# Causal softmax attention with heads of 8 channels: scores of two steps issued together, masked in PSUM, transposes two steps behind

## What is computed

```python
q, k, v = split((layernorm(x)) @ w_attn + b_attn)   # 16 heads of 8 channels
q, k = rope(q), rope(k)                             # pairs (2n, 2n+1) rotated
att = einsum("bhqd,bhkd->bhqk", q, k) / sqrt(8)
att = where(causal, att, -inf)                      # 256 x 256 for each of 256 (b, h)
y = einsum("bhqk,bhkd->bhqd", softmax(att), v)
x = x + y @ w_proj + b_proj
```

## Time and profile before

| | before |
|---|---|
| median of three runs | 2302.54 us |
| the profiled execution's own time | 2294.92 us |
| its span | 2293.1 us |
| mean granted TensorE clock, share of full | 0.978 |
| busy: TensorE / VectorE / ScalarE / GpSimd | 93% / 74% / 79% / 62% |
| the stage of the change, first S to last S | 209.1 to 523.3 us |

### The profile page before, as it was taken

How to read it: one execution, slowest core, us unless ns; L and a number is a source line. 1 busy time by engine, 2 the same in 40 slices (tenths; PEclk the granted TensorE clock), 3 DMA queues, 4 the chain that set the end, 5 groups by cost and what they waited for, 6 DMA issues and landing times. The chain is left out here.

```text
span 2293.1 us, 67424 instructions
## 1 busy us (share of the span) xinstructions
PE 2136.7 (93%) x22342; PEld 1585.6 (69%) x22342; DVE 1706.8 (74%) x4362; ACT 1801.0 (79%) x6112; POOL 1431.8 (62%) x1432
## 2 busy tenths in 40 slices
PE   6997999998797999999999999898999999999999
PEld 4994666665795888854888854674788864788863
DVE  5565999996555899964899964675899963899964
ACT  4775999995676999973999973556999982999982
POOL 3663777774662888840888850671788850788850
PEclk8997999999899999999999999999999999999999
DMA  6111000000113000000000000000000000000000
GB/s 249 44 42 42 2 0 0 0 1 38 35 44 111 12 7 9 7 3 3 11 7 9 7 0 0 2 0 6 9 9 8 8 1 5 9 9 7 9 1 37
DMA packets 22568, 46.02 MB, mean 20 GB/s; under 512 B 5344, under 2 KB 13664, under 8 KB 22048
## 3 DMA queue, kind: packets, MB, share of 16 engines
q1 hardware_dynamic: 17440, 34.07, 4.4%
q0 software_dynamic: 4992, 10.23, 1.6%
HBM read 24.51 MB, written 11.40 MB: 16 GB/s over the span
## 5 line engine op out<-in xcount | busy, mean ns | idle before, releaser
L280 POOL TENSOR_TENSOR space<-space 128x512 f32<-128x512 f32 x256 | 325.8, 1273 | 270.4 <-DVE space L383 270.1
L275 POOL TENSOR_TENSOR space<-space 128x512 f32<-128x512 f32 x256 | 267.6, 1045 | 128.1 <-ACT space L316 127.6
L330 ACT ACTIVATE space<-psum,space 128x128 f32<-128x128 f32 x1024 | 337.0, 385 | 2.7 <-DVE space L374 2.7
L177 PE MATMUL psum<-big,space 128*128 128x256 f32 x1024 | 267.9, 384 | 7.3 <-issue 3.5
L269 POOL TENSOR_TENSOR space<-space 128x512 f32<-128x512 f32 x256 | 267.0, 1043 | 7.9 <-DVE space L354 7.3
L1008 POOL TENSOR_TENSOR space<-space 128x256 f32<-128x256 f32 (+1 forms) x256 | 221.9, 888 | 75.2 <-DVE space L1117 70.9
L374 DVE TENSOR_REDUCE space<-psum 128x4 f32<-128x512 f32 x256 | 177.1, 692 | 100.8 <-PE psum L192 96.5
L1053 ACT ACTIVATE space<-space 128x128 f32<-128x128 f32 (+1 forms) x512 | 226.1, 446 | 7.3 <-DVE space L1108 6.5
L330 ACT ACTIVATION_READ_ACCUMULATOR space<-psum,space 128x1 f32 x1024 | 201.8, 197 | 0.0
L177 PEld LDWEIGHTS psum<-big,space 128*128 128x128 f32 x1024 | 175.6, 191 | 29.6 <-issue 16.2
L677 ACT ACTIVATE big<-psum,wt 128x512 f32<-128x512 f32 (+1 forms) x96 | 65.4, 686 | 151.9 <-PE psum L654 151.9
(11 more groups left out here) (194 smaller groups left out, 5425.8 us busy)
## 6 DMA issues: line engine op xcount, KB each, us to landing
big<-early SPq DMA_DIRECT2D x1, 6944.0 KB, 27.9
rows<-space SPq DMA_DIRECT2D x16, 256.0 KB, 2.7
z<-token_y SPq DMA_DIRECT2D x16, 256.0 KB, 4.7
space<-z SPq DMA_DIRECT2D x64, 64.0 KB, 1.9
space<-z SPq DMA_DIRECT2D x64, 63.8 KB, 2.1
big<-late SPq DMA_DIRECT2D x1, 3114.0 KB, 13.7
x<-x_t SPq DMA_DIRECT2D x4, 512.0 KB, 6.0
x_final<-x SPq DMA_DIRECT2D x8, 256.0 KB, 2.0
```

What stands on the lines that cost most here:

```text
L177: ins = mm(qk_ps[:, t * T:(t + 1) * T].rearrange("p (n c) -> p n c", n=2), hT[:, k, t * P:(t + 1) * P], wq[:, 0:2, j, :], start=(t == 0), ...
L275: pool.tensor_tensor(x, x, rn[:, (j - 1) % 2, :].unsqueeze(2).to_broadcast([P, 8, LD]), ALU.mult).then_inc(scaled, 1)
L280: pool.tensor_tensor(t3[:, j % 2, :], t1[:, j % 2, :], t2[:, j % 2, :], ALU.add).then_inc(summed, 1)
L330: ins = act.activation(pr[:, j % 2, h, t * P:(t + 1) * P], s_ps[h][:, t * P:(t + 1) * P], ACT.Exp, bias=nm[:, j % 2, h, t:t + 1], accum_ou ...
```

## The change

Five things change, all inside `small_head_softmax`:

1. TensorE issues S(s) and S(s+1) together in even steps. Neighbouring steps use different rows of the array.
2. M writes the masked scores back into the same PSUM banks, E reads them from there and writes `pr`, and the row sums `ls` lie in columns 384 and 385 of the same banks. The banks are therefore free only after R: S(s) waits for R(s-2) (`rl_ready`) and no longer for M(s-2).
3. ScalarE's order in an even step becomes E(s), E(s+1), H(s-2), H(s-1).
4. VectorE's order in an even step becomes R(s-1), M(s), M(s+1), L(s-2), R(s), L(s-1).
5. T runs two steps behind S: TensorE's order over two steps is S(s), S(s+1), T(s-2), T(s-1), PV for steps s-4 and s-3. The pair of banks `pt_ps` stays single.

```diff
+    ls = tuple(x[:, :, TRI:TRI + 2] for x in (g.bank_pair2, g.bank_pair4))
 # TensorE
+        def score(s, k, e):
+            jj, bank = e // 2, s_ps[e % 2]
...
+            if at_least(s, 2):
+                pe.wait_ge(rl_ready, s - 1)
+            for t, cols in ((0, slice(0, P)), (1, slice(P, TRI))):
+                for n in range(2):
...
+                    ins = mm(bank[n][:, cols], qz[r, k, jj, t * P:(t + 1) * P], qk[r, k, T:T + (t + 1) * P], start=(t == 0), stop=(t == 1), skip_group_check=True)
+            ins.then_inc(s_ready, 1)
+
         def body(i):
             for s, b, k, e in steps(i):
-                if runs(s, U):
-                    jj, bank = e // 2, s_ps[e % 2]
-                    if e % 2 == 0:
-                        pe.wait_ge(qz_ready, 4 * b + jj + 1)
...
-                    if at_least(s, 2):
-                        pe.wait_ge(nm_ready, s - 1)
...
+                if e % 2 == 0 and runs(s, U):
+                    pe.wait_ge(qz_ready, 4 * b + e // 2 + 1)
+                    score(s, k, e)
+                    score(s + 1, k, e + 1)
...
-                u = s - 3
+                u = s - 2
                 if runs(u, U):
-                    kk, ee = place(k, e, 3)
+                    kk, ee = place(k, e, 2)
                     pe.wait_ge(normed, u + 1)
 # ScalarE
+        def weights(u, ee):
+            act.wait_ge(nm_ready, u + 1)
+            if at_least(u, 4):
+                act.wait_ge(pt_ready, u - 3)
+            for t, (c0, c1) in enumerate(((0, P), (P, TRI))):
+                for h in range(2):
+                    ins = act.activation(pr[:, ee % SLOTS, h, c0:c1], s_ps[ee % 2][h][:, c0:c1], ACT.Exp, scale=-1.0,
+                                         bias=nm[:, ee % 2, t, h:h + 1], accum_out=ls[ee % 2][:, h, t:t + 1])
+            ins.then_inc(p_ready, 1)
+
+        def high(u, bb, ee):
+            act.wait_ge(pt_ready, u + 1)
+            if at_least(u, 4):
+                act.wait_ge(pv_ready, 4 * bb + ee // 2 - 1)
+            act.activation(pt[:, ee % SLOTS, 1, :], pt_ps[1][:, 0:TRI], ACT.Copy).then_inc(pt_high, 1)
+
         def body(i):
             for s, b, k, e in steps(i):
-                u = s - 1
-                if runs(u, U):
-                    kk, ee = place(k, e, 1)
-                    act.wait_ge(nm_ready, u + 1)
...
+                if e % 2 == 0 and runs(s, U):
+                    weights(s, e)
+                    weights(s + 1, e + 1)
+                if e % 2 == 0:
+                    ee = place(k, e, 2)[1]
+                    for n in range(2):
+                        if runs(s - 2 + n, U):
+                            high(s - 2 + n, of(b, e, 2), ee + n)
 # VectorE
+        def masked(u, ee):
...
+                    ins = dve.tensor_tensor_reduce(s_ps[ee % 2][h][:, c0:c1], s_ps[ee % 2][h][:, c0:c1], g.tri_q[:, c0:c1], -1.0, FAR,
+                                                   ALU.add, ALU.min, nm[:, ee % 2, t, h:h + 1])
...
+                    if runs(s - 1, U):
+                        inverse(s - 1, ee + 1)
+                    if runs(s, U):
+                        masked(s, e)
+                        masked(s + 1, e + 1)
+                    if runs(s - 2, U):
+                        low(s - 2, of(b, e, 2), ee)
+                    if runs(s, U):
+                        inverse(s, e)
+                    if runs(s - 1, U):
+                        low(s - 1, of(b, e, 2), ee + 1)
```

More of the change, by code:

```diff
@@ L872, in small_head_softmax @@
     s_ps = ((g.bank[2], g.bank[3]), (g.bank[4], g.bank[5]))
+    ls = tuple(x[:, :, TRI:TRI + 2] for x in (g.bank_pair2, g.bank_pair4))
     pt_ps = (g.bank[6], g.bank[7])
-    hT, xb, turn, qk, qz, vm, nm, ls, rl, pr = (room[x] for x in ("hT", "xb", "turn", "qk", "qz", "vm", "nm", "ls", "rl", "pr"))
+    hT, xb, turn, qk, qz, vm, nm, rl, pr = (room[x] for x in ("hT", "xb", "turn", "qk", "qz", "vm", "nm", "rl", "pr"))
     pt = g.z[:, 0:SLOTS * 2 * TRI].rearrange("p (s h n) -> p s h n", s=SLOTS, h=2)
@@ L919, in values @@
             ins.then_inc(vp_ready, 1)
+        def score(s, k, e):
+            jj, bank = e // 2, s_ps[e % 2]
+            if isinstance(s, int) and s < 2:
+                prev.free(pe, 2 + 2 * s)
+                prev.free(pe, 3 + 2 * s)
+            if at_least(s, 2):
+                pe.wait_ge(rl_ready, s - 1)
+            for t, cols in ((0, slice(0, P)), (1, slice(P, TRI))):
+                for n in range(2):
+                    q = 2 * (e % 2) + n
+                    r = slice(32 * q, 32 * q + 32)
+                    ins = mm(bank[n][:, cols], qz[r, k, jj, t * P:(t + 1) * P], qk[r, k, T:T + (t + 1) * P], start=(t == 0), stop=(t == 1), skip_group_check=True)
+            ins.then_inc(s_ready, 1)
         def body(i):
             for s, b, k, e in steps(i):
-                if runs(s, U):
-                    jj, bank = e // 2, s_ps[e % 2]
-                    if e % 2 == 0:
-                        pe.wait_ge(qz_ready, 4 * b + jj + 1)
-                    if isinstance(s, int) and s < 2:
-                        prev.free(pe, 2 + 2 * s)
-                        prev.free(pe, 3 + 2 * s)
-                    if at_least(s, 2):
-                        pe.wait_ge(nm_ready, s - 1)
[L932 to L937, removed]
+                if e % 2 == 0 and runs(s, U):
+                    pe.wait_ge(qz_ready, 4 * b + e // 2 + 1)
+                    score(s, k, e)
+                    score(s + 1, k, e + 1)
                 if runs(b + 1, B):
@@ L1062, in body @@
                     act.activation(tokens(g.hn, b - 1), ol, ACT.Identity, bias=bias[:, 2:3]).then_inc(out_ready, 1)
[L1063 to L1069, removed]
         biased(0)
@@ L1092, in queries @@
             dve.tensor_scalar(qz[:, k, jj, :], qk[:, k, 0:T], g.own8[:, jj:jj + 1], None, ALU.mult).then_inc(qz_ready, 1)
+        def masked(u, ee):
+            dve.wait_ge(v_zero, 1)
+            dve.wait_ge(s_ready, u + 1)
+            if at_least(u, 2):
+                dve.wait_ge(p_ready, u - 1)
+            for t, (c0, c1) in enumerate(((0, P), (P, TRI))):
+                for h in range(2):
+                    ins = dve.tensor_tensor_reduce(s_ps[ee % 2][h][:, c0:c1], s_ps[ee % 2][h][:, c0:c1], g.tri_q[:, c0:c1], -1.0, FAR,
+                                                   ALU.add, ALU.min, nm[:, ee % 2, t, h:h + 1])
+            ins.then_inc(nm_ready, 1)
@@ new lines, in inverse, with low @@
+        def inverse(u, ee):
+            dve.wait_ge(p_ready, u + 1)
+            if at_least(u, 2):
+                dve.wait_ge(normed, u - 1)
+            dve.reciprocal(rl[:, ee % 2, :, :], ls[ee % 2].rearrange("p h t -> p t h")).then_inc(rl_ready, 1)
+        def low(u, bb, ee):
+            dve.wait_ge(pt_ready, u + 1)
+            if at_least(u, 4):
+                dve.wait_ge(pv_ready, 4 * bb + ee // 2 - 1)
+            dve.tensor_copy(pt[:, ee % SLOTS, 0, :], pt_ps[0][:, 0:TRI]).then_inc(pt_low, 1)
@@ L1094, in body @@
         def body(i):
             for s, b, k, e in steps(i):
-                if runs(s, U):
+                if e % 2 == 0:
                     if not isinstance(s, int):
[L1098 to L1124, removed]
+                        for n in (-1, 0, 1, 2):
+                            dve.compute_val(s + n)
```

2 lines of the change are left out of this document (1 added, 1 removed).

## The result

| | before | after |
|---|---|---|
| median | 2303.85 us (4 runs, 2301.33 to 2312.95) | 2590.05 us (4 runs, 2587.03 to 2591.79) |
| profiled span | 2293.1 us | 2589.7 us |
| mean granted TensorE clock | 0.978 | 0.909 |

The ratio is 1.1233, 95% interval 1.1199 to 1.1266: slower by 286 us, as forecast in kind (+258 us, range 2445 to 2625). Nearly all of it lies in the changed stage: from the first S to the first product of the next layer the two profiles have 322.9 us (209.1 to 532.1) and 606.5 us (214.8 to 821.3). That is 283.5 us of the 296.6 us between the two spans; the other 13 us lie ahead of the stage (5.7) and behind it (7.3), where the code is the same. The page of the changed kernel: busy shares, then TensorE's busy tenths and granted clock in 40 slices of the span.

What follows compares the result with a forecast made beforehand. ScalarE set the pace before; the change makes a circle of waits bind. A sequence goes from 19.70 to 35.8 us: 16.1 more, times 16 = 258 us, on 2302.5 gives 2560 us, range 2445 to 2625.

Steps and rivals of the forecast that it cites:

- The circle and its links: In the changed stage E(s), E(s+1), H(s-2), T(s-1), PV, S(s+2), M(s+2) each wait for the one before, once a pair.
- Its length: The waits from E to the next pair's E sum to 7.22 us at full clock, 9.21 at half, against 4.93 before.
- M in place: VectorE's masking, reading and writing the same PSUM bank, was taken to cost zero more than writing SBUF.
- The clock: TensorE's granted clock in the stage goes up and down, a quarter of the time at full: 35.8 us a sequence.
- Rival 1: The circle of waits in the stage runs at full clock throughout: +163 us, 2466 us; chance 0.17.
- The exponentials' gain: On ScalarE a step's four exponentials, reading PSUM with sums there, fall from 1.77 to about 1.40 us.
- M still 1.1 us: Sign of being right: in the changed kernel's profile, VectorE's M still takes 1.1 us a step.
- the other stages' time stays: Sign of being right: the time of all stages outside the changed one is unchanged.
- The paired S at nothing: On TensorE S(s+1) is nearly free beside S(s), about 0.9 us a pair at full clock, counted at nothing.
- PV waiting for the output: Once a sequence PV in step 5 waits for ScalarE's output, standing behind H(s-1): 1.0 us a sequence.

Runs made afterwards that it cites:

- e1: Changed kernel with ScalarE's even-step order H(s-2), E(s), E(s+1), H(s-1), so H(s-2) comes ahead of both E: 2488.3 us, ratio 1.0823.
- e3: Changed kernel with GpSimd's N leaving out its second product (rows that see 256 keys not normalized): 2582.63 us, ratio 1.1233.
- e10: Kernel before with ScalarE's order alone changed: E(s-1), E(s) together in even steps, then H(s-3), H(s-2): 2508.48 us, ratio 1.0898.
- e4: Changed kernel with 14 useless TensorE products of 128 x 128 added ahead of T(s-1): 2505.51 us, ratio 1.0898.
- e5: Changed kernel with masked scores and sums back in SBUF, all orders as changed: 2605.53 us, ratio 1.1322.
- e8: Kernel before with S(s) and S(s+1) issued together in even steps, nothing else changed: 2296.66 us, ratio 0.9995.
- e11: Kernel before with T, L and H two steps behind S instead of three: 2385.26 us, ratio 1.0347.
- e6: Kernel before with scores and sums in PSUM alone, S waiting for R(s-2), all orders as before: 2333.83 us, ratio 1.0136.
- e7: e2 with five useless TensorE products of 128 x 128 added between T(s-2) and T(s-1): 2459.41 us, ratio 1.0710.
- e2: e1 with VectorE's order M(s), L(s-2), M(s+1) in place of M(s), M(s+1), L(s-2): 2471.25 us, ratio 1.0744.
- e9: e2 with masked scores and sums in SBUF as in e5, S(s+1) waiting for M(s-1): 2420.8 us, ratio 1.0500.

## Why the prediction was right

- **The circle and its links**: right. The walk through the rows above, e1 and e3 show it, and e10 shows that ScalarE's new order closes a circle of this kind by itself, with TensorE's order as before; the forecast had not said that.
- **Its length**: 0.5 us short. By the rows after, at half clock: M to E 524.32 - 522.92 = 1.40 (said 1.22), two E 2.85 (2.80), H and hop 0.80 (0.57), T 529.41 - 527.97 = 1.44 (1.47), PV 1.44 (1.35), S to M 522.92 - 521.12 = 1.80 (1.80); 9.73 against 9.21. The misjudged terms are M in place, taken at zero from the earlier trace rows, where a 512-column operation showed no dearer write, and H, which lasts 0.65 behind eight exponentials and 0.49 alone. Both lie on the circle, 0.18 and 0.23 a pair, together 26 us in 64 pairs. The sum can be tested: the pair at half clock took 9.72 (above). With T, PV and S to M at full clock the same links give 7.68, and the pair of e4 from 436.99 to 444.67 took 7.68.
- **The clock**: right in kind, a quarter of the time at full was a bit low. A mean of 0.68 means 36% at full. Errors of length and clock partly cancelled: 4 x 9.73 + 1.0 = 39.9 us at half, 32.4 at full (e4), mixed 64 to 36 gives 37.2, and 37.5 was measured. Luck had a part: the two errors had opposite signs, and what is left of them is most of the 28 us missed.
- **Rival 1** (circle at full clock, 2466 us) lies 40 us below e4's 2505.51; the circle's length, 0.46 a pair, makes 29 of them. The clock in the changed kernel was not at full, so the rival didn't happen.
- **The exponentials' gain**: right. Four take 525.76 - 524.32 = 1.44 us (said 1.40). The scores in PSUM as a whole, dearer M included, were worth 15 to 20 us inside the circle (e5).
- **M still 1.1 us**, which the prediction named as a sign of being right: wrong, it is 524.27 - 522.92 = 1.35. Its sign that the other stages' time stays is right but for 13 us of 2000 in the two profiles.
- **The paired S at nothing**: right (e8).
- **PV waiting for the output**: right, 1.0 us a sequence. The list of waits of the changed kernel over two sequences (us, times, longest):

```profile
PE psum L979 <- ACT hn L1081: 2.1, 2, 1.0
```

- **Missed altogether**: the lag of two, +80 us by itself (e11), and the hold of the banks until R, which with the dearer M is +31 us by the ratio (e6) and makes a circle of its own in e7. Both were hidden behind the first circle, so they didn't disturb the forecast (T(s-2) at 524.06 follows S without a wait), and they spoiled the expectations for e2, e7 and e9. So did PV's wait for the output: priced at 1.0 us for the changed kernel, it grew to 2.65 in e7 and 3.36 in e9.

## What to carry to other kernels

Before regrouping in-order queues "by twos", write down for each single buffer who must empty it, what stands ahead of that on its own queue, and whether that in turn waits for what stands behind the buffer's next user; such a circle costs the sum of its links however idle each engine is. Here ScalarE's order in twos cost 203 us by itself, and cheaper exponentials, some 47 us in the prediction if ScalarE set the pace, were worth 15 to 20 with the dearer M once the pace was set by waits. Removing one circle shows the next: test each part of a bundled change alone on the kernel before, because undoing them one by one only uncovers what lay hidden.

## What the runs showed of the hardware that was not expected

- M in place in PSUM is dearer than into SBUF: 466 and 322 ns for 256 and 128 columns in the changed kernel (two sequences, grouped by form), and the accumulator's read 142 ns; the same groups of the kernel before have 416, 282 and 80.

```profile
L1113 DVE CUSTOM_DVE_ANT_0 psum<-psum,cb 128x256 f32<-128x256 f32 x32 | 13.6, 466 | 0.0
L1113 DVE DVE_READ_ACCUMULATOR2_ANT space<- 128x1 f32 x64 | 9.1, 142 | 0.0
L1113 DVE CUSTOM_DVE_ANT_0 psum<-psum,cb 128x128 f32<-128x128 f32 x32 | 9.0, 322 | 12.6 <-issue 12.6
```

- The share of time in which TensorE is recorded busy does not tell its clock: e10 had 48.98 of 60.00 us busy and a clock of 0.72, e11 (below) 51.83 of 60.00 and 0.84, while e8 had 15.44 of 20.00 and 1.00. Half clock itself makes the busy time longer (T takes 1.54 us at 524.06 in the changed kernel and 0.85 in the earlier trace rows), so a low clock can look like a busy engine.

```profile
400.00:460.00 60.00, 51.83 (x432) 33.90 (x430) 44.79 (x208) 43.94 (x179) 36.45 (x43) 0.84 0.00 0
```

- Fourteen small products of no use in each waiting gap made the changed kernel 85 us faster (77 by the ratios): the granted clock was 1.00 in place of 0.68, and the links after the gap ran at full clock.
